# Where the two-pass steps stand in the order of a feature-interaction kernel

## The reference

```
z0   = einsum('bid,bjd->bdij', x, x)          # 39 x 39 products for each b, d
cur0 = relu(einsum('bdk,kl->bld', z0, W0))     # W0: (1521, 128)
next_h, direct0 = split(cur0, 2, axis=1)       # 64 rows each
z1   = einsum('bid,bjd->bdij', x, next_h)      # 39 x 64 products
cur1 = relu(einsum('bdk,kl->bld', z1, W1))     # W1: (2496, 128)
z    = sum(concat([direct0, cur1]), axis=-1)   # then joined with 16 dense features
y    = relu(relu([z, dense] @ W_top1 + b1) @ W_top2 + b2) @ W_top3
```

## Time and profile before

| | |
|---|---|
| median of 3 runs | 1530.21 us (1529.78 to 1533.06) |
| profiled execution | 1528.59 us |
| its span, first to last instruction | 1526.8 us |
| busy, PE / DVE / ACT / POOL | 1445.1 / 1397.4 / 824.2 / 978.0 us |
| mean granted clock of TensorE | 0.978 of full speed |
| chain that ended last: PE, DVE, issue | 52%, 31%, 11% |

### The profile page before, as it was taken

One profiled execution on the slowest core, in us unless ns is written; L12 is line 12 of the kernel. 1 busy time (PEld: TensorE's weight loads), 2 busy tenths in 40 slices (PEclk: granted clock), 3 DMA queues, 4 the chain that ended last, 5 costly groups with the idle time before them and its releaser, 6 DMA issues.

```text
span 1526.8 us, 15137 instructions
## 1 busy us (share of the span) xinstructions
PE 1445.1 (95%) x4484; PEld 798.2 (52%) x4484; DVE 1397.4 (92%) x1325; ACT 824.2 (54%) x893; POOL 978.0 (64%) x604
## 2 busy tenths in 40 slices
PE   3179999999999999999999999999999999999999
PEld 2145555555555555555555555555555555555556
DVE  2279999999999999999999999999999999999971
ACT  0056555665655555565565555565565555565644
POOL 7648888878687886878687886878687880000000
PEclk7589999999999999999999999999999999999999
DMA  4069999899998989899999999899998898889600
GB/s 145 6 160 206 231 216 210 213 208 219 209 212 207 214 213 208 214 206 215 208 214 207 219 206 213 212 206 220 220 209 201 214 209 213 210 203 202 176 1 1
DMA packets 137258, 292.93 MB, mean 192 GB/s; under 512 B 37630, under 2 KB 62862, under 8 KB 137048
## 3 DMA queue, kind: packets, MB, share of 16 engines
q1 hardware_dynamic: 102610, 278.31, 77.2%
q0 software_dynamic: 19200, 4.95, 3.0%
q10 hardware_dynamic: 15366, 8.70, 2.1%
HBM read 283.95 MB, written 7.87 MB: 191 GB/s over the span
## 4 chain that ended last, share of the span: by engine, by line
PE 52%; DVE 31%; issue 11%; another core or an unknown queue 3%; DMA 1%; SPq 0%; DVEq 0%; ACT 0%
PE psB L477 23%; DVE z L859 12%; DVE z_lo L868 8%; PE psA L477 8%; DVE z_split L859 8%; PE psB L502 4%; PE psB L495 3%; PE psB L498 3%; DVE r L921 2%; PE psA L485 2%; PE psB L485 1%; PE psA L495 1%; PE psA L502 1%; PE psA L498 1%
## 5 line engine op out<-in xcount | busy, mean ns | idle before, releaser
L456 POOL DMA_INDIRECT emb<-in_tbl,ids_all x600 | 977.8, 1630 | 279.8 <-issue 178.6
L477 PE MATMUL psB<-z,w 128*128 128x512 f32 x1536 | 685.8, 592 | 5.0 <-DVE z L859 3.0
L734 ACT ACTIVATE z_hi<-z_split 128x1024 fp32r<-128x1024 f32 (+1 forms) x288 | 303.8, 1058 | 483.1 <-DVE z_split L859 416.9
L477 PEld LDWEIGHTS psB<-z,w 128*128 128x128 f32 x1536 | 291.0, 190 | 359.9 <-issue 340.4
L859 DVE TENSOR_TENSOR z<-h_quad,x_lay 128x1024 f32<-128x1024 f32 x352 | 417.5, 1215 | 5.9 <-PE psB L477 4.4
L868 DVE TENSOR_TENSOR z_lo<-z_split,z_hi 128x1024 fp32r<-128x1024 f32 (+1 forms) x288 | 351.1, 1219 | 3.9 <-ACT z_hi L734 3.9
L859 DVE TENSOR_TENSOR z_split<-h_quad,x_lay 128x1024 f32<-128x1024 f32 x224 | 270.9, 1221 | 0.0
L689 ACT ACTIVATE h_quad<-psA 32x1024 f32<-32x1024 f32 x248 | 251.4, 1014 | 3.7
L477 PE MATMUL psA<-z,w 126*128 126x512 f32 x512 | 240.7, 592 | 0.5 <-issue 0.5
L495 PE MATMUL psB<-z_hi,w_hi 128*128 128x512 f32 x448 | 158.8, 436 | 0.2 <-issue 0.2
L502 PE MATMUL psB<-z_lo,w_hi 128*128 128x512 f32 x448 | 141.7, 398 | 7.7 <-DVE z_lo L868 6.6
(11 more groups left out here) (102 smaller groups left out, 859.2 us busy)
## 6 DMA issues: line engine op xcount, KB each, us to landing
x_lay<-x_rows SPq DMA_DIRECT2D x1152, 128.0 KB
x_more<-x_rows SPq DMA_DIRECT2D x62, 504.0 KB
bases<-x_rows SPq DMA_DIRECT2D x62, 468.0 KB
x_lay<-x_rows SPq DMA_DIRECT2D x64, 256.0 KB
x_ring<-x_rows SPq DMA_DIRECT2D x31, 504.0 KB
emb<-in_tbl,ids_all POOLq DMA_INDIRECT x600
x_last<-x_rows SPq DMA_DIRECT2D x64, 128.0 KB
x_rows<-x_side ACTq DMA_DIRECT2D x58, 120.0 KB
```

The source lines that it names most:

```text
L456: nc.gpsimd.indirect_dma_start(emb[t % 2][:, f * D:(f + 1) * D], None, tables[f], bass.IndirectOffsetOnAxis(ids_all[:, t, f:f + 1], 0)).th ...
L477: mm = nc.tensor.matmul(ps[:, cs], w[0:k, :], z[WHOLE_NO[place] % NZ][0:k, cs], start=first, stop=last)
L734: nc.scalar.activation(z_hi[n % NS][0:k, 0:cols], z_split[n % NS][0:k, 0:cols], ACT.Copy).then_inc(z_hi_made, 1)
```

## The change

Layer 0 has three split steps, 1, 3 and 5, in place of 1 and 4; layer 1 has six, 3, 4, 7, 8, 13 and 14, in place of seven, 2, 3, 7, 8, 9, 13 and 14. There are nine in a unit either way. The order of places stays. At the start of the run, where ACT's list is written out for unit 0, a third `high` is added.

```diff
-SPLIT0 = (1, 4)
+SPLIT0 = (1, 3, 5)
 HALF1 = 12
-SPLIT1 = (2, 3, 7, 8, 9, 13, 14)
+SPLIT1 = (3, 4, 7, 8, 13, 14)
@@
             high(at0(0, SPLIT0[0]))
             keep_part(4, more[2][0:ROWS, :], half(psB, 0))
+            high(at0(0, SPLIT0[1]))
             keep_half(5, half_a, half(psB, 1))
             keep_half(6, half_b, half(psA, 1))
             act.wait_ge(part_spread, 5)
             spread_x(1)
-            high(at0(0, SPLIT0[1]))
+            high(at0(0, SPLIT0[2]))
             keep_x(1)
```

## The result

The changed kernel took 1557.49 us (median of 4 runs, 1553.56 to 1559.72) against 1530.01 for the kernel before: a ratio of 1.0166, 95% interval 1.014 to 1.0192. Its profiled execution took 1559.72 us with a span of 1557.6. The page first, then the half steps that mark the units, as in rows 3 (timeline of PE: start and length in us).

A forecast was written before the change was run, and what follows sets the result against it. PE and DVE were taken as nearly equally busy (95% and 92%), PE waiting for z_lo at line 502. 29 × 1.0 + 0.4 − 9.5 + 0 = +20 us, so 1530.2 + 20 = 1550 us; range 1538 to 1556.

The forecast's parts named there:

- Work unchanged, no price for alternating on PE: Per period PE, DVE and ACT do the same instructions, and more changes between whole and split steps cost PE nothing.
- The walk behind the turn: From the first of the four transposes to layer 0 step 5's late line 502: 0.97 us per period, taken as 1.0.
- The wait of the copy behind keep_x: On ACT, step 1.4's z_hi copy queues behind keep_x and two DMA issues, starting 2.49 us after keep_x.
- bind there by 0.48: In the longest period ACT's wait puts step 1.4's z_lo at 804.73, where DVE alone would be there at 804.25.
- The third rival: ACT's wait is harmless, DVE alone decides: three in four periods lose 0.5 us; +1.5 in all, 1532 us; chance 0.06.
- 0.58 gained: Layer 0's step 5 split has one more whole step ahead: PE gives 1.72 us, DVE uses 1.135, 0.58 in favour.
- The trio: DVE's split multiplication, whole multiplication and z_lo in a row with ACT's copy exposed: 3.49 to 3.51 us, lower bound 3.41.
- The first rival: The wait behind keep_x binds but ACT's copies hide, three DVE instructions taking 3.41 us: +9, 1539 us; chance 0.11.
- 9.5 us is all that a better order can win: Steady part: 29 periods exceed PE's own work of 42.47 us each by 9.5 us in all, the most to win.
- The second rival: The stalls vanish and interleaving wins: all periods 42.47 us, −9.5, 1520.7 us; chance 0.11.
- Start and end: Added copy on ACT at the start +1, one split fewer in unit 31 −1: together 0, bounds −1 to +2 us.

The follow-up runs named there:

- the second: The changed kernel run again with no edit, against the kernel before on the same chip: 1519.43 against 1497.24 us, ratio 1.0143.
- eight spread splits: Changed kernel with step 4 of layer 1 whole again, so eight split steps per unit, against the kernel before: 1493.69 against 1497.02 us, ratio 0.9978.
- extra activation: One unused ACT activation added behind each keep_x from unit 3 on: changed kernel 1539.35 us, ratio 1.0286 to the kernel before; kernel before with it 1496.27, ratio 1.0002.
- keep_x moved: Changed kernel with keep_x behind the copy of layer 1's step 4 in ACT's list, except unit 0: 1510.96 against 1496.61 us before, ratio 1.0107.
- the copies hidden: Changed kernel with keep_x behind the step 1.4 copy and each z_lo two places behind its product: 1553.67 us, ratio 1.0413; with 27 of 39 gathers 1491.49, 0.9983.

## Why the prediction held, point by point

The forecast was slower by 20 us, range 1538 to 1556; measured were 27.5 more in the first comparison and 22.2 in the second. The first time, 1557.5, lies 1.5 us above the range's upper end, and the 6.6 us of the first period, which I had not foreseen, put it there. The forecast of slower and most of its size came from the repeating part, 22.0 us in 28 periods for an expected 19.9 in 29.

*Work unchanged, no price for alternating on PE.* Right: the same counts, and 42.85 us periods with eight spread splits.

*The walk behind the turn.* Right to 0.2 us: L(1.4) at 4.33 for 4.21, L(0.5) at 18.35 for 18.17, line 502 at 19.63 for 19.44. The period is 42.47 + 1.1 = 43.58 for an expected 43.47. Twenty-nine times 0.1 is the 2 to 3 us that the repeating part was short. But the walk starts from the assumption that ACT's item sets the time in every unit, and that was so in light ones only.

*The wait of the copy behind keep_x.* Right as a mechanism (extra activation: 0.80 in every period, 0.01 in the kernel before), but in the heavy units it was not what set the period. I let it bind there by 0.48; taking it away gave back 0.05 to 0.23. I had S(0.1) at 14.27 behind the half step, from the earlier trace rows. In the changed kernel it is at 814.77 − 799.89 = 14.88: DVE's lead over PE is 0.6 shorter, which fits the last L, one place nearer to the half step. So keep_x starts behind the copy of S(1.3) (820.61, its end is 820.59) and not at the turn's 0.64, and DVE's own pace and the queue come to nearly the same time. That they do was luck: the forecast needed only one of them to be right, and had DVE's own lateness in the heaviest unit as 0.97 − 0.48 = 0.49 over 42.47, where with keep_x moved it is 43.65 − 42.47 = 1.18. Taken alone, the queue item is 0.36 per period and the exposed copies 0.42. The third rival, DVE alone, is off by the same term: it had heavy periods 0.5 over 42.47 and +1.5 us in all; with keep_x moved they are 0.82 to 1.18 over it, and the total is 14 us over the kernel before. The term that was wrong in both is DVE's own time in a heavy unit. Its walk took the W more ahead of S(0.5) as 0.58 gained and kept S(0.1) where it had been; in heavy units neither held, and their periods rose by the whole price of the five copies, 0.50 to 0.57.

*The trio.* I took 3.49 to 3.51 from the earlier trace rows; it is 3.51 to 3.52. The first rival (copies hide, 3.41) is ruled out for this order.

*"9.5 us is all that a better order can win".* True as a bound for PE and of little use. The late line 502 of the earlier trace rows was the sign of a deficit and not its cause. In heavy units DVE waited for nobody: from 780.65 to 823.80 it was busy for 43.02 of 43.15 us, and the profile lists no wait of it. Its waits of four periods all stand in the light one:

```profile
DVE z L859 <- PE psB L477: 1.5, 3, 0.6
DVE z_lo L868 <- ACT z_hi L734: 0.3, 1, 0.3
```

So only fewer exposed copies, 0.1 us each, could shorten a heavy period, and the change has five more. The second rival (1520.7) could not happen for this reason; the trace of before showed it, had I listed DVE's waits in a heavy period. What interleaving needs is room on the less loaded engine; here DVE waited for 1.8 us in four periods of 171.2, and not at all in three of the four.

*Start and end.* The start came to +1.4 for an expected +1, in part by luck: 0.8 of it are there before the first product (the copy to x_ring starts at 85.76 and not at 84.98, cause open), and the third `high` gives some 0.7 (DVE waits 1.40 for ACT ahead of the last z_lo of that stretch, 0.67 before). The end came to +0.8 and not −1. The first period's 6.6 us I did not foresee (loads, which I held to be unchanged); it did not come back in the experiments, and its cause stays open.

## What to carry to other kernels

When two engines are nearly level, spreading the expensive steps can help only if the engine that feeds has idle time in the same period; look for its gaps before counting the other's stalls. (With room in every period, eight splits, the order was worth nothing here either.) Each time a producer, a helper and the producer again form a chain (multiply, copy, subtract), a lone one exposes the helper's latency and a group hides all but the first. And before a step that needs a helper engine is moved, read that engine's list at the new place: a handshake with a third engine and two DMA issues were free where nobody waited behind them and cost 0.36 us a unit where a copy did, and 0.80 more with one item more.

## What the runs showed of the hardware

A gather on POOL took 0.95 us while DVE was idle and 1.97 while it ran without a gap. The 1.97 and the 0.30 behind each are 2.27, twice the 1.135 from one DVE instruction to the next. Between 200 and 1300 us of the run, without the six long ones, the mean is 1.65 in the kernel before, 1.43 after (DVE has small gaps there) and 1.69 to 1.78 with the copies hidden.

The long ones, one in four units, differ much more: 7.0 us before and after, 16.1 with z_lo one place later on the kernel before, up to 41.2 with the copies hidden. Where I looked, they start around DVE's sum of finished units and end close to the next break in its row of products: the one of the kernel before lasts from 791.06 to 798.09, with DVE's first late instruction at 797.25, and the one of 16.1 from 772.30 to 788.41, with DVE's first idle time, 0.28 us, ahead of 787.87. Such a gather takes the time of some twenty others from POOL, and that made POOL the bound. The Trainium skill (SBUF — State Buffer, SBUF: two separate sides) says that a DVE operation with two inputs in SBUF and a GpSimd operation that reads SBUF exclude each other for a whole instruction. The doubled gathers fit that, and so would a gather that gets no turn while DVE has no gap; no run here shows the lock itself, nor why only one gather in four units is held so long.
